# Attention order by batch: batch 0's routing placed among batch 1's attention blocks in a one-core attention and mixture-of-experts kernel

## The reference, cut to what matters

```python
x = (x - mean) * rsqrt(var + EPS) * g + b          # context, and tokens likewise
q = lat @ Wq
kv = concatenate([x, lat], axis=1) @ Wkv           # 1101 keys and values per batch
out = softmax(q k^T / 8) v ; return out @ Wout     # 16 heads
...
x = x + attention
h = layernorm(x)
shared = (silu(h @ sg) * (h @ su)) @ sd
# routing: best 4 of 8 groups, best 4 of their 32 experts, softmax of the 4 scores
pos = cumsum(onehot over all tokens) - 1           # place of a token in its expert
keep = pos < 320
# each expert: 320 slots, silu(b @ wg) * (b @ wu) @ wd, added back with its gate
return x + shared + routed
```

## Time and profile before

| | |
|---|---|
| time, 3 runs | 1681.18 us median, 1678.7 to 1681.22 |
| profiled execution | span 1731.2 us, the only time there is of it |
| PE busy | 1541.0 us, 89% of the span |
| DVE, ACT, POOL busy | 999.6, 800.9, 939.7 us |
| DMA queue of SP | 93.82 MB |
| DMA queue of POOL | 19.97 MB |

### The profile page before, as it was taken

How to read it: one execution, slowest core, us unless ns; L and a number is a source line. 1 busy time by engine, 2 the same in 40 slices (tenths; PEclk the granted TensorE clock), 3 DMA queues, 4 the chain that set the end, 5 groups by cost and what they waited for, 6 DMA issues and landing times.

```text
span 1731.2 us, 25990 instructions
## 1 busy us (share of the span) xinstructions
PE 1541.0 (89%) x8078; PEld 1075.6 (62%) x8078; DVE 999.6 (58%) x1517; ACT 800.9 (46%) x1548; POOL 939.7 (54%) x748
## 2 busy tenths in 40 slices
PE   2799999999999999999999998853488999999995
PEld 1555555555555555555555555442477999999995
DVE  5455565565565565565565565483135666666663
ACT  2344544544544544544544544431125666666663
POOL 3366676676676676676676676535701334343433
PEclk8799999999999999999999999856798999999998
DMA  9600000000000000000000000022305667676664
GB/s 228 138 14 10 14 14 10 14 13 9 13 13 9 13 13 9 13 13 9 13 13 9 14 13 1 1 93 84 116 24 169 182 176 187 166 192 171 183 173 92
DMA packets 92700, 114.28 MB, mean 66 GB/s; under 512 B 10195, under 2 KB 71637, under 8 KB 92629
## 3 DMA queue, kind: packets, MB, share of 16 engines
q1 hardware_dynamic: 75605, 93.82, 18.8%
q0 software_dynamic: 17056, 19.97, 5.9%
HBM read 71.78 MB, written 35.06 MB: 62 GB/s over the span
## 4 chain that ended last, share of the span: by engine, by line
PE 80%; DVE 7%; ACT 5%; issue 3%; another core or an unknown queue 3%; DMA 1%; POOL 0%; SPq 0%; DVEq 0%; ACTq 0%; POOLq 0%
PE ps_o L832 15%; PE ps_t L720 9%; PE ps_m L794 9%; PE ps_st L817 8%; PE ps_m L720 8%; PE ps_st L720 7%; PE ps_st L821 6%; ACT arena L1458 3%; PE ps_t L857 3%; PE ps_o L913 3%; PE ps_m L913 3%; PE ps_t L844 2%; PE ps_t L939 2%; PE ps_t L800 1%
## 5 line engine op out<-in xcount | busy, mean ns | idle before, releaser
L636 POOL TENSOR_TENSOR arena<-arena 128x512 f32<-128x512 f32 (+1 forms) x512 | 656.3, 1284 | 370.9 <-ACT arena L1458 346.8
L1458 ACT ACTIVATE arena<-ps_st 128x512 f32<-128x512 f32 (+1 forms) x576 | 326.3, 595 | 434.9 <-PE ps_st L821 420.9
L1246 DVE TENSOR_REDUCE arena_r<-ps_m 128x1 fp32r<-128x1101 f32 x256 | 332.3, 1298 | 234.4 <-PE ps_m L794 230.7
L678 POOL DMA_INDIRECT acc_rows<-arena,ids x96 | 151.8, 1581 | 315.7 <-ACT arena L1555 288.2
L817 PE MATMUL ps_st<-arena_r 128*128 128x512 f32 (+1 forms) x576 | 262.6, 456 | 24.2 <-ACT arena L1458 24.2
L832 PE MATMUL ps_o<-arena 128*64 128x512 f32 (+1 forms) x1152 | 268.4, 601 | 0.0
L821 PE MATMUL ps_st<-arena_r 68*128 68x512 f32 (+2 forms) x576 | 229.6, 399 | 0.9 <-DVE arena_r L1253 0.9
L794 PE MATMUL ps_m<-arena_r 128*128 128x512 f32 (+1 forms) x768 | 193.0, 360 | 6.3 <-DVE arena_r L1246 6.3
L794 PEld LDWEIGHTS ps_m<-arena_r 128*128 128x128 f32 x768 | 134.6, 192 | 102.7 <-issue 44.6
L817 PEld LDWEIGHTS ps_st<-arena_r 128*128 128x128 f32 (+1 forms) x576 | 106.9, 186 | 111.9 <-ACT arena L1458 87.9
L1507 ACT ACTIVATE arena<-ps_m 128x320 f32<-128x320 f32 (+1 forms) x144 | 65.7, 456 | 234.6 <-PE ps_st L720 166.8
(11 more groups left out here) (175 smaller groups left out, 1802.7 us busy)
## 6 DMA issues: line engine op xcount, KB each, us to landing
arena<-in_L_ffn_wg_dram SPq DMA_DIRECT2D x32, 512.0 KB
arena<-in_L_ffn_wu_dram SPq DMA_DIRECT2D x32, 512.0 KB
arena<-in_L_ffn_wd_dram SPq DMA_DIRECT2D x32, 512.0 KB
x_slots<-arena SPq DMA_DIRECT2D x5, 2176.0 KB, 19.9
arena<-x_slots SPq DMA_DIRECT2D x32, 272.0 KB, 2.7
arena_r<-arena_r SPq DMA_DIRECT2D x30, 275.2 KB, 3.6
arena<-x_slots SPq DMA_DIRECT2D x32, 68.0 KB, 2.4
x_sb<-in_x_dram SPq DMA_DIRECT2D x2, 1024.0 KB, 7.4
```

Of the source, the lines that this page charges most:

```text
L636: pool.tensor_tensor(acc, probsT[0:rows, h, 0, :] if kt == 1 else acc, probsT[0:rows, h, kt, :], ALU.add).then_inc(added, 1)
L678: pool.indirect_dma_start(out=dst[:, :], in_=y_sb[par][:, c, 0:w], in_offset=None, compute_op=ALU.add, out_offset=bass.IndirectOffsetOnAxi ...
L1246: dve.tensor_reduce(neg[h][:, c:c + 1], scores_m[:, 0:KEYS], AX.X, ALU.max, negate=True)\
L1458: act.activation(probsT[0:rows, h, kt, :], ps_st[0:rows, n % 2, :], ACT.Exp)\
```

## The change

A turn of attention now takes two pairs of heads of one batch (`pp` 0 and 1), two blocks each. Turns 0 to 3 are batch 0, turns 4 to 7 are batch 1. Each pair's weights are therefore loaded and split twice, once for each batch. One list `whole_plan` holds everything from the first projection to the last shared chunk, all engines run through it, and all of it is written out: no hardware loop is left before the experts. In detail:

- The start loads batch 0 in two halves, and only batch 0 and the context rows are normalised and turned ahead of the first projection. Each half's high and low parts are made from PSUM (`split_kv`). Batch 1's statistics (`bstat`) stand in the prologue, between batch 0's projections and the first maxima; its normalising (`zs`), turning (`zt`) and splitting (`zl`) stand in turns 1 to 3.
- The five zero fills of `x_slots` are issued one by one in turns 0 and 1 (`fill`).
- The routing goes in groups of 512 tokens (4 tiles). Groups 0 and 1 (batch 0) stand in turns 4 to 7, their 32 scatters in turns 5, 6 and 7. Groups 2 and 3 follow the attention. The squares (L1469) are gone: the norm comes from the variance.
- The shared weights' load and split start in turn 7's last block. The shared expert's chunk 0 can start before batch 1 is routed. The routing of group 3 stands between chunks 0 and 1.
- The first expert's weights are split during chunk 3 (`ws1`), and an expert's weights go in three pieces instead of four.

The diff is cut to the plan and to what the steps below speak of; the programs of the engines follow the plan event by event with the same instructions as before, except where a line is shown.

```diff
+def extra_events():
+    for j, (T, d) in enumerate(((0, 1), (0, 2), (0, 3), (1, 0), (1, 1))):
+        put(T, d, 0, 6, ("fill", j))
+    put(0, 0, 0, 4, ("cenn",))
+    for i, (T, d) in enumerate(((1, 2), (2, 0), (2, 2), (3, 0))):
+        put(T, d, 0, 7, ("zs", i))
+        put(T, d, 1, 7, ("zt", i))
+        put(T, d, 1, 8, ("zl", i))
+    put(4, 0, 0, 6, ("stat", 0))
+    put(4, 1, 0, 1, ("stat", 1))
+    put(4, 1, 0, 6, ("root", 0), ("root", 1))
+    for g, (T, d) in enumerate(((4, 2), (6, 2))):
+        put(T, d - 1, 1, 7, ("normed", g))
+        put(T, d, 0, 1, ("turned", g, 0))
+        put(T, d, 0, 2, ("low", g, 0))
+        put(T, d, 0, 5, ("turned", g, 1))
+        put(T, d, 0, 6, ("low", g, 1))
+        put(T, d, 0, 7, ("score", g))
+        put(T, d, 1, 0, ("top", g))
+        put(T, d, 1, 1, ("mask", g))
+        put(T, d, 1, 5, ("best", g))
+        put(T, d, 1, 8, ("hot", g))
+        put(T, d + 1, 0, 1, ("gexp", g))
+        put(T, d + 1, 0, 6, ("gates", g))
+        put(T + 1, 0, 0, 4, ("pos", g))
+        put(T + 1, 0, 0, 7, ("places", g))
+    spots = [(0, 2), (0, 7), (1, 2), (1, 7)]
+    for i in range(SCATTERS):
+        put(5, 1 + i // 4, *spots[i % 4], ("scat", 0, i)) if i < 12 else put(6, 0, *spots[i % 4], ("scat", 0, i))
+        put(7, 0, 1, (1, 3, 5, 8)[i], ("scat", 1, i)) if i < 4 else put(7, i // 4, *spots[i % 4], ("scat", 1, i))
+    put(LAST_T, LAST_D, 1, 6, ("wload",))
+    put(LAST_T, LAST_D, 1, 7, ("stat", 2))
+    put(LAST_T, LAST_D, 1, 8, ("root", 2), ("ws", 0), ("ws", 1))
+    return extra
...
+    tail = end[:3] + [("normed", 2), end[3], ("turned", 2, 0), ("turned", 2, 1), ("low", 2, 0), ("low", 2, 1),
+                      end[4], ("ws", 2), ("score", 2), end[5], end[6], ("stat", 3), ("root", 3)]
+    tail += ups(0, 0, 1) + [("top", 2), ("mask", 2), ("normed", 3), ("turned", 3, 0), ("turned", 3, 1),
+                            ("low", 3, 0), ("low", 3, 1), ("best", 2), ("hot", 2), ("gexp", 2)]
+    tail += ups(0, 2, 3) + [("score", 3), ("pos", 2), ("gates", 2), ("places", 2)] + scats[2]
+    tail += [("low_hid", 0), ("down", 0), ("top", 3), ("mask", 3), ("best", 3), ("hot", 3), ("gexp", 3), ("accout", 0)]
+    tail += ups(1, 0, 1) + [("pos", 3), ("gates", 3), ("places", 3)] + scats[3] + ups(1, 2, 3)
+    tail += [("low_hid", 1), ("down", 1), ("accout", 1)]
+    tail += ups(2, 0, 1, 2, 3) + [("low_hid", 2), ("down", 2), ("accout", 2)]
+    tail += ups(3, 0) + [("ws1", 0)] + ups(3, 1) + [("ws1", 1)] + ups(3, 2) + [("ws1", 2)] + ups(3, 3)
+    tail += [("low_hid", 3), ("down", 3), ("accout", 3)]
...
-            attend(FIRST, 0)
-            with dve.Fori(1, HP - 1) as turn:
-                attend(TURN, turn)
-            attend(FINAL, HP - 1)
-            attend(END, HP)
+            for ev, T in PLAN:
...
+                if kind == "root":
+                    g = a
+                    act.wait_ge(var_ready, stats_in + g + 1)
+                    h = slice(g * GT, (g + 1) * GT)
+                    act.activation(std[:, h], mv[:, h, 1], ACT.Sqrt, bias=eps[:, :]).then_inc(std_ready, 1)
+                    act.activation(rnorm[:, h], mv[:, h, 1], ACT.Sqrt, scale=float(D)).then_inc(std_ready, 1)
+                    if g == 1:
+                        act.preload_act_table(ACT.Exp)
...
+                if kind == "scat":
+                    _, g, i = ev
+                    if i == 0:
+                        pool.wait_ge(slots_ready, g + 1)
+                        if g == 0:
+                            pool.wait_ge(init_out, 32 * FJ)
```

More of the change, by code:

```diff
@@ L49, with turn_slots @@
 KEY_TILES = 9
-PROJECT = [("k", 0), ("k", 2), ("k", 1), ("q", 0), ("q", 1)]
+TURNS = 8
+TURNS_B = TURNS // 2
+GROUPS = 4
+GT = 4
 LAST_D = QUADS - 1
-IN_RING = ("k", "q", "v", "row", "sum", "out")
-JOB_OF_TURN = {("k", 0, 0): ("turned", 0, 0), ("k", 0, 2): ("turned", 0, 1), ("k", 0, 1): ("turned", 1, 0),
-               ("q", 0, 0): ("turned", 1, 1)}
-TURN_OF_JOB = {turned: job for job, turned in JOB_OF_TURN.items()}
-def attention_plan():
-    turn = []
+LAST_T = TURNS - 1
+FILLS = 5
+SCATTERS = GT * 4
+WPIECES = 3
+HIDS = 4
+def turn_slots():
+    slots = []
     for d in range(QUADS):
@@ L122, in attention_plan @@
             for kt in range(KEY_TILES):
-                turn += [own("st", d, h, kt)] + ([own("add", d, h, kt)] if kt else []) + after.get((h, kt), [])
-    before = [("w", 0)]
-    for i in (0, 2, 1):
-        before += [("k", 0, i), ("hi", "k", 0, i, (0, 1)), ("lo", "k", 0, i)]
-    before += [("q", 0, 0), ("hi", "q", 0, 0, (0, 1)), ("hi", "q", 0, 0, (2, 3)), ("v", 0, 0), ("max", 0, 0, 0),
-               ("lo", "q", 0, 0), ("v", 0, 1), ("max", 0, 0, 1), ("v", 0, 2), ("max", 0, 0, 2), ("max", 0, 0, 3),
-               ("row", 0, 0)]
@@ L157, in d_of @@
-    def d_of(events):
-        return max((ev[1] for ev, back in events if ev[0] == "st"), default=0)
-    first = [item for ev, back in turn for item in ([(ev, back)] if back < 1 else stand_in(ev, back))]
-    final = [item for ev, back in turn for item in ([(ev, back)] if back >= 0 else stand_in(ev, back))]
-    final = stand_in_router(final)
-    end = [item for item in turn if item[1] == 1] + [(("gap", ("pad",)), 1)]
-    at = [ev[0] for ev, back in end]
-    end.insert(at.index("sum") + 1, (("stat", 2), 1))
@@ L166, in attention_plan, with put @@
-    end.insert(at.index("sum") + 2, (("score", 0), 1))
-    return before, first, turn, final, end
+                slots.append([own("st", d, h, kt)] + ([own("add", d, h, kt)] if kt else []) + after.get((h, kt), []))
+    return slots
+def extra_events():
+    extra = {}
+    def put(T, d, h, kt, *events):
+        extra.setdefault((T, d, h, kt), []).extend(events)
+    for j, (T, d) in enumerate(((0, 1), (0, 2), (0, 3), (1, 0), (1, 1))):
[31 more added lines that the diff above has]
+    return extra
@@ new lines, in whole_plan, with ups @@
+def whole_plan():
+    before = [("w", 0), ("kv", 0), ("zn",), ("k", 0, 0), ("hi", "k", 0, 0, (0, 1)), ("q", 0, 0), ("kv", 1),
[3 rows of a table added]
+              ("max", 0, 0, 1), ("v", 0, 1), ("max", 0, 0, 2), ("v", 0, 2), ("max", 0, 0, 3), ("row", 0, 0)]
+    plan = [(ev, 0) for ev in before]
+    slots, extra = turn_slots(), extra_events()
+    ahead = [ev for slot in slots for ev, back in slot if back == -1]
+    assert set(ahead) <= set(before), set(ahead) - set(before)
+    for T in range(TURNS):
+        for slot in slots:
+            for ev, back in slot:
+                if 0 <= T - back < TURNS:
+                    plan.append((ev, T - back))
+                elif T == 0 and ev[0] == "out":
+                    plan.append((("cen", ev[2]), 0))
+            plan += [(ev, T) for ev in extra.get((T,) + slot[0][0][1:], [])]
+    end = [ev for slot in slots for ev, back in slot if back == 1]
+    assert [ev[0] for ev in end] == ["av"] * 3 + ["sum", "norm", "out", "out"]
+    scats = [[("scat", g, i) for i in range(SCATTERS)] for g in range(GROUPS)]
+    def ups(c, *hts):
+        return [("up", c, ht) for ht in hts]
+    tail = end[:3] + [("normed", 2), end[3], ("turned", 2, 0), ("turned", 2, 1), ("low", 2, 0), ("low", 2, 1),
[9 more added lines that the diff above has]
+    tail += [("low_hid", 3), ("down", 3), ("accout", 3)]
+    return plan + [(ev, LAST_T) for ev in tail]
@@ L170, in xattn_moe @@
+JOB_KINDS = ("k", "q", "v", "row", "sum", "out", "cen", "zt", "turned", "score", "pos")
 def xattn_moe(nc, x, ctx_in, ln_m_g, ln_m_b, ln_l_g, ln_l_b, Wq, Wkv, Wout, group_c, expert_c, e_bias,
@@ L325, in xattn_moe @@
+        route = sb("route", [P, GT * (GE + 3 * E + G)])
+        carve = carver(route)
+        sc = carve(GT * GE, "p (t g) -> p t g", t=GT)
+        masked, chosen, before = (carve(GT * E, "p (t e) -> p t e", t=GT) for _ in range(3))
+        gmask = carve(GT * G, "p (t g) -> p t g", t=GT)
+        fill = route[0:FP, 0:2 * RW].rearrange("p (j d) -> p j d", j=2)
+        z_two = route[:, 0:2 * D].rearrange("p (t d) -> p t d", t=2)
         ident = sb("ident", [P, P])
@@ L660, in _ @@
[L660 to L668 removed]
+            seq.done(pool.memset(fill[:, :, :], 0.0))
```

1512 lines of the change are left out of this document (722 added, 790 removed), and 3 rows, old and new, of the table before.

## The result

The changed kernel takes **1703.6 us** (median of 4 runs, 1698.8 to 1706.96), the kernel before 1680.6: a ratio of 1.0136, interval 1.0117 to 1.0155. The forecast was 1664, and 1703.6 lies just above the upper end of its range (1703). The rival *the attention pays for it* said 1710.

A forecast was written before the change was run, and what follows sets the result against it. PE was taken to bound the attention loop and the experts. Terms -20 - 15 + 5.5 + 10 + 15 + 8 - 21 = -17.5 took 1681.2 to 1664 us; own range 1645 to 1684, whole range 1630 to 1703.

The forecast's parts named there:

- the attention pays for it: Rival, chance 0.18: in the attention DVE waits for POOL and PE for DVE, +61 instead of +15, 1710 us.
- The cleaned time: Stretch from attention to last shared chunk: 185.1 us profiled, taken as 133 in timed runs without 52 of scatter stalls.
- stalls are real: Rival, chance 0.17: stalls beside scatters occur in timed runs too, so -47 instead of -21 after the attention, 1638 us.
- The start: Start to first finished score: batch 1's preparation and other work leave the path, -20 us, bounds -12 and -25.
- the start stays: Rival, chance 0.10: small inputs or batch 1's statistics set the first score, the -20 nearly gone, 1684 us at most.
- Turn 7: Last attention turn: time lost to batch 0's preparation goes, -15 us, bounds -10 and -18.
- Written-out code: Attention: twelve half turns leave the hardware loop at 0.46 us each, +5.5 us, bounds -5 and +8.
- PE's moved work: Attention: transposes, router scores and places moved in where PE has no idle time, +10 us, bounds 8 and 12.
- DVE's moved work: Attention: 41 us of routing and batch 1 work moved in, costing +15 us, bounds 0 and 61.
- POOL: Attention: scatters ahead of POOL's scaling make it late for PE, +8 us, bounds 0 and 20.
- After the attention: Last score to last shared product: 112 us instead of the cleaned 133, -21, bounds -40 and -8.
- Experts: Expert stage: three weight pieces instead of four hold the same columns, 0 us, bounds -2 and +3.

The follow-up runs named there:

- the second profile: The kernel before, unchanged, profiled once more: span 1677.0 us, own time 1678.8 us.
- late_routing: Changed kernel with groups 0 and 1 prepared, routed and scattered wholly after the last score; 1725.76 us, ratio 1.0267 to the kernel before.
- reslotted_2: Changed kernel with batch 1's, routing and scatter pieces at other places, 8 of group 1's scatters after the attention; 1645.15 us, 0.9799 of before.

## Why the prediction was wrong, by its own steps

- **The cleaned time.** Right. 133 us were worked out for the middle stretch without stalls, 133.04 were measured. The rival *stalls are real* falls. Its reason, the profiler beside a burst of scatters, was wrong: the kernels with bursts and the second profile show no gap.
- **The start**, -20: measured -16.6 against the second profile and -18.3 against the earlier trace rows. Right; the rival *the start stays* falls.
- **Turn 7**, -15: low end. In late_routing, with only statistics and roots at its very end and no scatters, the stretch is 65.35 + 66.99 = 132.3 instead of 143.06, so -10.7. The estimate gave too little time for the last half.
- **Written-out code**, +5.5: (65.27 - 64.87) x 12 = +4.8. Right. The rule of the Trainium skill that speaks for unrolling (Runtime: NRT & Kernel Launch, Instruction fetch mechanics) is not borne out here: the written-out half turns are the longer ones.
- **PE's moved work**, +10: 0.4 x 4 + 2.8 x 2 + 0.6 x 2 = 8.4 from the busy times of half turns at a clock of 1.00. Right.
- **DVE's moved work**, +15. **This step failed.** What the attention's +62.6 (1106.6 against 1044.0) leaves for it, without 0.7 in turn 0, 4.8, -10.7, 8.4 and the scatters' 8.3, is 51 us (its share of the slower clock included) where 15 was said. Three of its parts were wrong. Batch 1's pieces were put at 1; they cost 11.5 with 1.6 of PE, because the normalising stands ahead of a row that has 1.4 us to spare and takes 2.91 us instead of 0.73. `best` and `hot` were put at 0; PE waits 1.14 and 2.03 for them. `top` and `mask` were put at 3; PE waits 4.64. The 1.2 us of slack at that maximum was read from a block without the weight split; with the split 0.44 is left. Two of the lines are locked besides, and the clock falls after the wait.
- **The same step, what it left out.** The lock stood only in the upper bound, though the earlier trace rows showed it, and there on an instruction that, against the rule as it was used, has one large input (L1088). The work itself was put too low as well: DVE is busy for 71.9 us more in the attention than before, 9.9 of turn 7 have gone, so some 82 came in, and still 63 in reslotted_2, where little is lengthened, against the 41 of the forecast.
- **The choice between the bounds.** The upper bound, 61 from turn 7's 1.5 us per us, was nearer. It was set aside with the argument that small pieces with whole slots between them lose less. The runs show that the line that follows decides more than the size: the same 3.5 us cost 3.1 or nothing. The rival's point was 0.8 us per us, 32.5 in all; 51 is past it, 1.2 for each of the 41 us (0.8 for each of the measured 63). The rival *the attention pays for it* is the one that came true, its time 6 us too high.
- **POOL**, +8: the size was right (1.6 + 1.7 + 5.0 = 8.3), the way only in part. Not the scaling was the price in turn 5, but the weight split behind a scatter (2.88 us) and the maximum behind it.
- **After the attention**, -21: -19.7. **Experts**, 0: -0.4. Both right.

Of the announced signs, the first score (52.8), the stretch of 112 (113.3) and the experts held. Turns 1 and 3, with one piece of batch 1 each, took 133.0 us and so held too; turn 2, with two, took 137.1, over the 133.8 allowed. Turns 4 and 6 were longer by 21 and 19 where 7 to 10 was said, and crossed the 145 us that were to prove the forecast wrong (69.39 + 82.12 = 151.5).

## What to carry to other kernels

When work is pushed into a loop that one engine bounds, the busy share of the helping engine says nothing: read for each place which instruction comes next on that engine and how long before the bound engine's request it ends, and read it in the very block, for the slack here was 1.2 us in one and 0.4 in another. Nearly the same instructions made this attention 63 us longer at one set of places and 7 at another (8 of 32 scatters had left it). Price an instruction that was lengthened anywhere in the trace by its longest row, keep it out of slots that it could overrun, and leave something for the clock behind the bound engine's waits: 4.5 us in the half turn of 82.
